# The turned second layer for the rectified mixture too, and the context mask's parts behind items 11 and 12

## The reference

```python
# layer 0, the rectified mixture: 8 experts, D = 128, F = 512
logits = h @ gate_w + gate_b            # the two largest of 8 get weight 1, the others 0
y = sum(w[:, e] * (relu(h @ w1[e] + b1[e]) @ w2[e] + b2[e]) for e in range(8))
x = x + y
# then layer 1: x = x + sliding_attention_block(layernorm(x)), then
#               x = x + cross_attention(ctx, layernorm(x), mask)   <- uses the context mask
```

## Time and profile before

| what | value |
|---|---|
| runs | 962.81 us median of 3 (961.25 to 965.34) |
| the profiled execution | 958.12 us, span of its instructions 954.9 us |
| PE busy | 888.6 us, 93% |
| VectorE busy | 673.0 us, 70% |
| ScalarE busy | 542.1 us, 57% |
| GpSimd busy | 354.6 us, 37% |
| mean granted clock of TensorE | 0.989 |

### The profile page before, as it was taken

The page is one execution under the profiler, slowest core; times in us unless marked ns, Lnnn a source line. Parts: engine busy times, 40 slices in busy tenths (PEclk is TensorE's granted clock), DMA queues, the critical chain, the costliest instruction groups (busy, mean ns, idle before and its releaser), DMA issues.

```text
span 954.9 us, 16573 instructions
## 1 busy us (share of the span) xinstructions
PE 888.6 (93%) x6182; PEld 679.7 (71%) x6182; DVE 673.0 (70%) x1311; ACT 542.1 (57%) x1228; POOL 354.6 (37%) x446
## 2 busy tenths in 40 slices
PE   7998999999989899999888889999989999989998
PEld 4556889985576597887444437777878976678787
DVE  6887743558868857865899985656677575854784
ACT  1765434437634567855788763545547455734784
POOL 4852189955326400012388982211000053420000
PEclk9999999999999999999999999999999987999999
DMA  6610011100001004303000001000000000000420
GB/s 125 193 48 13 1 45 45 34 23 2 2 1 46 12 3 133 99 1 132 1 1 0 0 1 45 1 1 2 1 2 1 1 1 1 1 13 23 133 79 22
DMA packets 35201, 30.74 MB, mean 32 GB/s; under 512 B 3948, under 2 KB 28848, under 8 KB 34867
## 3 DMA queue, kind: packets, MB, share of 16 engines
q1 hardware_dynamic: 35123, 29.70, 10.7%
HBM read 29.10 MB, written 0.59 MB: 31 GB/s over the span
## 4 chain that ended last, share of the span: by engine, by line
PE 70%; DVE 13%; POOL 7%; ACT 5%; issue 4%; DMA 0%; POOLq 0%; SPq 0%; DVEq 0%; ACTq 0%
PE banks L950 15%; PE banks L975 14%; POOL work L1836 4%; PE banks L373 4%; PE banks L364 4%; PE banks L1626 3%; DVE work L543 2%; PE banks L2005 2%; PE banks L396 2%; PE banks L990 2%; PE banks L989 2%; PE banks L994 2%; DVE work L535 2%; ACT work L2209 2%; PE banks L2016 2%
## 5 line engine op out<-in xcount | busy, mean ns | idle before, releaser
L1058 ACT ACTIVATE work<-banks,keep 128x512 f32<-128x512 f32 x236 | 157.2, 688 | 124.9 <-PE banks L950 124.7
L950 PE MATMUL banks<-rounded 128*128 128x512 f32 x672 | 169.8, 398 | 1.2 <-DVE rounded L1182 0.6
L975 PE MATMUL banks<-keep,work 128*128 128x128 f32 x1248 | 148.6, 275 | 0.7 <-ACT work L1058 0.6
L975 PEld LDWEIGHTS banks<-keep,work 128*128 128x128 f32 x1248 | 146.1, 192 | 4.2 <-DVE keep L1213 0.8
L950 PEld LDWEIGHTS banks<-rounded 128*128 128x128 f32 x672 | 122.2, 188 | 29.6 <-issue 3.5
L709 ACT ACTIVATE work<-banks,work 128x128 f32<-128x128 f32 (+1 forms) x448 | 121.5, 388 | 30.7 <-DVE work L535 28.5
L150 POOL TENSOR_TENSOR keep<-keep 128x4 f32<-128x4 f32 x26 | 26.7, 1029 | 215.2 <-DVE keep L129 185.3
L1213 DVE SCALAR_TENSOR_TENSOR keep<-banks,keep 128x128 f32<-128x128 f32 x176 | 49.7, 344 | 63.9 <-PE banks L975 63.0
L535 DVE TENSOR_REDUCE work<-banks 128x8 f32<-128x1024 f32 (+1 forms) x64 | 68.8, 1077 | 29.0 <-PE banks L364 27.9
L1836 POOL TENSOR_TENSOR work<-work,keep 128x1024 f32<-128x1024 f32 x31 | 73.1, 2375 | 40.3 <-DVE work L1766 30.7
L1626 PE MATMUL banks<-work,keep 128*128 128x512 f32 x128 | 61.7, 606 | 13.5 <-POOL work L1836 11.9
(11 more groups left out here) (336 smaller groups left out, 1671.2 us busy)
## 6 DMA issues: line engine op xcount, KB each, us to landing
keep<-in_L_ffn_w_dram SPq DMA_DIRECT2D x32, 256.0 KB, 3.5
keep<-in_L_ffn_W_dram SPq DMA_DIRECT2D x16, 256.0 KB, 4.3
shared<-gelu_gate_rows SPq DMA_DIRECT2D x10, 256.0 KB, 3.8
shared<-gate_gate_rows SPq DMA_DIRECT2D x10, 256.0 KB, 3.7
shared<-in_L_xattn_Wkv_dram SPq DMA_DIRECT2D x1, 2048.0 KB, 8.2
shared<-in_L_ffn_expert_w_dram SPq DMA_DIRECT2D x8, 128.0 KB, 2.5
shared<-in_L_ffn_expert_w_dram SPq DMA_DIRECT2D x1, 1024.0 KB, 7.5
keep<-in_L_attn_conv_w_dram SPq DMA_DIRECT2D x1, 1024.0 KB, 7.7
```

Source lines behind the costliest of these rows:

```text
L950: m = pe.matmul(k.ps[:, c, :], w[:, c * P:(c + 1) * P], x[:, h * HALF:(h + 1) * HALF], start=j == 0, stop=j == len(parts) - 1)
L975: m = pe.matmul(k.ps[:, self.bank(n, j), j * P:(j + 1) * P], self.hT[n % 2][:, c, j * P:(j + 1) * P], w2[c], start=c == 0 and self.kind != ...
L1058: act.activation(self.hT[n % 2][:, c, :], k.ps[:, c, :], self.func, bias=bias, scale=scale)\
```

## The change

The rectified mixture joins the other two: experts 2 to 6 (items 4 to 12 and 14) take `layer2_across`, with the gates' way through DRAM, the splits of w2, the two turns of the sum, and a DRAM tensor for its gates. Two of the four buffers of spread gates lie on the biases' blocks (`blocks[:, 0, ...]`) of this mixture, so SP waits for `b2_done` before it spreads. `gated`, the scratch of the products, moves to the second half of `xnT`, since the first half is written early by the turn of n3. The buffers of the high parts lie over the place of the mask's parts, so the mask is made behind item 11 and its parts behind item 12, when item 11's layer 2 is over. The spins at the attention's start move from bank 7, where the sum is turned, to bank 4, and wait for item 14's product.

```diff
-            spin(k, pe, MB, 1)
+            pe.wait_ge(*self.mixture.acc_done.upto(self.mixture.items - 1))
+            spin(k, pe, PT0, 1)
...
-            spin(k, pe, *{"self": (MB, 8), "context": (OB, 6), "packed": (MB, 16)}[self.kind])
+            spin(k, pe, *{"self": (PT0, 8), "context": (OB, 6), "packed": (MB, 16)}[self.kind])
...
-        self.across = range(2, 7) if kind in ("gelu", "gate") else ()
+        self.across = range(2, 7) if kind in ("relu", "gelu", "gate") else ()
...
             if e == 4 and self.across:
                 self.store_gates(sp)
+                if self.kind == "relu":
+                    sp.wait_ge(*self.b2_done.upto(1))
                 for n in range(4, 8):
                     self.spread_gate(sp, n)
...
-        k.gate_rows = {n: nc.dram_tensor(n + "_gate_rows", (8, B, S), F32).ap() for n in ("gelu", "gate")}
+        k.gate_rows = {n: nc.dram_tensor(n + "_gate_rows", (8, B, S), F32).ap() for n in ("relu", "gelu", "gate")}
...
-        k.gated = k.xnT[:, 0:HALF]
+        k.gated = k.xnT[:, HALF:TOK]
...
-        l1_attn = Attention(k, n3, t3, "self")
+        l1_attn = Attention(k, n3, t3, "self", mixture=l0_ffn)
...
-            if n == 6:
+            if n == 11:
                 setup.vector_mask(dve)
-            if n == 8:
+            if n == 12:
                 setup.vector_mask_parts(dve)
```

More of the change, by code:

```diff
@@ L206, with __init__ @@
     STEPS = 2 * B
-    def __init__(self, k, norm, turn, kind, setup=None, behind=None):
+    def __init__(self, k, norm, turn, kind, setup=None, behind=None, mixture=None):
         self.k, self.norm, self.turn, self.kind = k, norm, turn, kind
-        self.setup, self.behind = setup, behind
+        self.setup, self.behind, self.mixture = setup, behind, mixture
         self.H = 8 if kind == "context" else 16
```

## The result

The changed kernel takes 966.87 us (median of 20 runs, 963.31 to 969.19), the kernel before 953.33 in as many runs beside them (949.01 to 965.34): ratio 1.014, 95% interval 1.0116 to 1.0164, so slower by 13.5 us. Some executions of a kernel, at a lower granted clock, are over 1.5% longer than its fastest, and the ratios leave those out. The three runs of before that were shown ahead of the prediction lie at the upper end of its spread. The profiled execution took 965.95 us, its span is 964.2 (before: 958.12 and 954.9). Lines from about 830 on are three higher than before: L950 is L953, L975 is L978, L1142 is L1145, L1161 is L1164, L2573 to L2575 are L2576 to L2578, L2515 is L2518.

What follows compares the result with a forecast made beforehand. PE bounds the first mixture now; after the change GpSimd's queue decides. Its lateness, +9.2 us with the PE gain and mask delay vanishing in the wait, plus 3.5 of clock gives +12.7: 975.5 us on a 962.81 median, range 965 to 982.

Steps and rivals of the forecast that it cites:

- The forecast case: First mixture: late GpSimd makes PE wait, +9.2 us, plus 3.5 of clock; total 975.5 us, chance 0.70.
- Part 1: PE's work in the first mixture: the turned second layer shortens the stretch from 73.70 to 66.90 us, -6.8.
- Part 2: Gates through DRAM on SP's queue: one store, ten spreads; waits for them and for the biases are covered, cost 0.
- Part 3: ScalarE's and VectorE's added work per turned item: VectorE still waits 0.68 us per item, so PE loses nothing.
- Part 4: Mask moved behind items 11 and 12: by VectorE alone the last item starts 3.7 us later than in gelu's timetable.
- Part 5: GpSimd's roundings ahead of n3's power end at 206.4, 13.7 us later, by walking them over VectorE's operations; time +9.2 us.
- Part 6: PE's clock falls behind its idle time before the last item: 0 to 5 us more, taken as 3.5.
- GpSimd keeping its pace: Rival: first mixture's roundings end before about 194, so the mask's place sets the end; 959.7 us, chance 0.11.
- VectorE is held as well: Rival: VectorE's SBUF operations in the first mixture wait too, about 7.0 us per item; about +11, 974 us, chance 0.10.
- Full gain: Rival: the mask and GpSimd's work in the first mixture are both hidden; 956 us, chance 0.04.
- worse: Rival: slowed VectorE and GpSimd add up and the clock stays low into the attention; 985 us, chance 0.05.
- The rule weighed in the prediction: Skill's rule: VectorE and GpSimd share a port lock held per instruction, second comer fully blocked; VectorE would lose like GpSimd.

Runs made afterwards that it cites:

- experiment 8: Changed kernel with 27 wide roundings and both pooled sums behind the first cross attention, mask rows behind item 1, parts split behind items 11 and 12: 943.09 us, ratio 0.9923.
- experiment 10: As experiment 8, but with the two pooled sums behind the 27 moved roundings instead of ahead of them: 942.89 us, ratio 0.9901.
- the control: Kernel before, with the 27 wide roundings and both pooled sums moved behind the first cross attention's GpSimd work: 952.05 us, ratio 0.9996.
- experiment 5: Changed kernel with the 27 wide roundings and both pooled sums moved behind the first cross attention's GpSimd work: 948.13 us, ratio 0.9963.
- experiment 9: Changed kernel with the mask alone moved, rows behind item 1 and parts split behind items 11 and 12: 968.15 us, ratio 1.0173.
- experiment 3: Changed kernel with the second subtraction of each pair in the first mixture waiting on a semaphore for the first: 963.45 us, ratio 1.0121.
- Experiment 1: Changed kernel with GpSimd's two pooled sums moved behind the cross attention of layer 1: 961.92 us, ratio 1.0106.
- experiment 2: Changed kernel with the 27 roundings of width 256 moved behind the first cross attention's GpSimd work: 950.46 us, ratio 0.9989.
- Experiment 4: Changed kernel with 88 unread spin matmuls on PE in the wait ahead of the turn of n3's first half: 973.11 us, ratio 1.0219.
- experiment 7: Changed kernel with all 81 roundings moved behind the first cross attention's GpSimd work, the pooled sums left in place: 954.38 us, ratio 1.0021.

## Why the prediction was right

The forecast case came: slower, because GpSimd is late, by +13.5 us in the medians and +14.7 in the stage, against +12.7. That the sum is so near is in part luck, because two of its terms missed in opposite directions: GpSimd's lateness by +3.8 and the clock by -2.4, which makes 14.1; the stage's first row lies 0.65 earlier in the changed profile, which makes the stage's 14.7. The time was missed by 8.6 us: 966.87 against 975.5, and 1.9 above the lower end of the range, because of the base. Term by term:

- **Part 1, right.** "66.90 - 73.70 = -6.8": the stage without waits measured 67.21 and 67.23 (experiments 8 and 10), and the control kept 73.70. It is worth -6.5.
- **Part 2, right.** PE has no wait for the spreads, and the only wait for a DMA is VectorE's 0.2 us.
- **Part 3, right in its price, and the cover was thinner than I wrote.** PE never waits in the items, but VectorE's 0.68 us of idle time per item is gone from 161 on, where GpSimd's operations lengthen its own (L1168 0.84 for 0.69, casts 0.61 for 0.43).
- **Part 4, right in direction, its size too large.** "The last item starts 3.7 us later than in gelu's timetable": with GpSimd's work out of the way (experiment 5) the turn waited 1.57 us. The parts took 5.1 us without roundings beside them, where I had used the 6.15 of before, and those were measured beside roundings; they also began 0.5 us earlier than in my timetable. In the changed kernel itself it vanished in the wait, as said: moving the mask alone gained nothing (experiment 9).
- **Part 5, right in mechanism, 3.8 us too small.** Forecast: last rounding at 206.4; measured 210.2. The step that was mis-sized is "about 0.7 us of wait in the first and 0.5 in the second": the walk let GpSimd in between the two subtractions. An operation with one tensor input isn't let in when the second follows without a gap, and then stands through both: 2.63 to 3.17 us for operations of 0.72 and 1.22. For L2578, with two, the walk was right in the turn, and had no term for what VectorE loses by it (0.27 us). With the gap put in, the end is at 206.9 (experiment 3). Behind the rounding all went as written: two sums, the power without idle time before it, four normals. Experiment 1 shows the chain one for one, and experiment 2 gives back more than the whole loss.
- **Part 6, 2.4 us too large.** I took 3.5 of a span from 0 to 5, from the row of another stage. The changed kernel lost 1.1: the clock was at 0.50 for 3.1 us only. Experiment 4 confirms it with 1.0. (In experiments 1, 3 and 9 the same place, from L182 to L41, lost 2.0, 2.5 and 1.5, within the bounds.)
- **The base.** 975.5 was worked out from a median of 962.81 of three runs; over 20 runs before's median is 953.33. The profiled execution, 4.7 below that median, had been the better guide; the difference of the two kernels is what the working gave, and that is 0.8 off.

**The rivals.** GpSimd keeping its pace is refuted by the rows at 144.48 and 172.52. "VectorE is held as well" happened in small and without effect on PE: four of the stage's nine pairs took 2.58 to 2.73 us instead of 2.35, sums and casts 0.15 to 0.4 more, and the items still stay at 5.55 us. Its price is real, and showed as soon as the pooled sums came to lie beside the items (experiment 2) or beside the normals (experiment 7). "Full gain" came once the roundings, the sums and the mask had moved (experiments 8 and 10); "worse" did not come.

**The rule weighed in the prediction.** The row that the prediction set against it was misread: L1182 at 142.83 began 0.09 us before GpSimd's operation at 142.92, so it came first, and its 0.69 us say nothing against the rule. These rows of before do, of VectorE and of GpSimd:

```profile
123.32 0.74 DVE L1182 TENSOR_TENSOR rounded<-keep,rounded 128x512 fp32r<-128x512 f32 x1
```
```profile
122.87 1.00 POOL L2573 TENSOR_SCALAR work<-shared,keep 128x128 f32<-128x128 f32 x1
```

GpSimd's operation, with one tensor input, had begun 0.45 us earlier and ran to 123.87, yet L1182 took only 0.05 us more than alone. The changed kernel shows it again: L1153, which began at 171.46 behind a rounding that had begun at 171.26 and ran for 1.27 us, took 0.93 us for its 0.69, so it did not wait for that rounding's end. Beside L2518 or L2519 (two SBUF tensors in) it is VectorE that waits to GpSimd's end and a little more. The Trainium skill, SBUF — State Buffer, section "SBUF: two separate sides", has one exclusive lock, held for a whole instruction, with the loser blocked fully. For the operations with two tensor inputs the trace agrees (2.79 and 4.56 us), and likewise for GpSimd when it comes second; that VectorE got through beside a rounding which had started first does not fit it, and here the measurement decides.

## What to carry to other kernels

When work goes to VectorE, look at what GpSimd does beside it and at what is queued behind that: here a free queue of 81 small roundings, with 3.26 us to spare, became the critical path, and moving 27 of them to a place with room took the whole loss away; with the two sums and the mask moved too, the change is a gain of 1%. Price an operation of GpSimd by the gaps that VectorE leaves, not by its length alone; for a GpSimd operation with one tensor input, two VectorE subtractions without a gap between them are one block. And a long GpSimd operation with two inputs should not start beside VectorE work that PE needs soon (in experiment 2 VectorE lost 4.3 us and PE waited 2.2 of them), nor become free to start earlier because something ahead of it was moved (experiment 7).

## What the runs showed of the hardware

- A GpSimd operation with one tensor input that begins during a VectorE subtraction with two SBUF inputs waits for the last of a gapless pair: 3.17 us for 1.22, 2.75 for 0.72. One with two tensor inputs gets its turn between the two: 0.96 us for 0.46, and the second subtraction takes 1.48 us for 1.22. A gap of 0.09 us between the two let the first kind in as well and brought the roundings' end 3.2 us forward.
- In the other direction, GpSimd's sum of 128x1024 with two inputs holds VectorE: a subtraction of 0.69 us took 2.79, four normals of 1.11 together took 5.23. The latter have one tensor input and a column of scalars; the first two of them took 2.30 and 2.49 us, beside L2518 and L2519, and the others 0.33.
- The clock behind a wait doesn't follow the wait's length: 1.57 us of idle time cost 1.6 us of clock in experiment 5, 1.44 us at the same place cost nothing in experiment 2 (L978 stayed at 1.96), and 19.78 us cost 1.1. Busy spins kept it at 1.00 through 20 us. Two of that kernel's four executions were some 10 us longer, and the profiled one of them had a long episode at 0.50 to 0.67 some 100 us later; a kernel without spins has such an episode too (0.57 from 300 to 340, experiment 8), so what brings it on stays open.
